# A graph attention kernel on one core: lookups of 128 edges with edges on partitions in place of edges on columns

## What is computed

```python
def _tconv(x, src, dst, ea, Wq, bq, Wk, bk, Wv, bv, We, Ws, bs):
    q = (x @ Wq + bq).reshape(n, H, C)
    k = (x @ Wk + bk).reshape(n, H, C)
    v = (x @ Wv + bv).reshape(n, H, C)
    e = (ea @ We).reshape(-1, H, C)
    kj = k[src] + e
    alpha = jnp.einsum('ehc,ehc->eh', q[dst], kj) / jnp.sqrt(jnp.float32(C))
    amax = jax.ops.segment_max(alpha, dst, num_segments=n)
    ex = jnp.exp(alpha - amax[dst])
    denom = jax.ops.segment_sum(ex, dst, num_segments=n)
    w = ex / (denom[dst] + 1e-16)
    msg = (v[src] + e) * w[:, :, None]
    out = jax.ops.segment_sum(msg, dst, num_segments=n).reshape(n, D)
    return out + x @ Ws + bs

x = _layernorm(x + _L0_gnn_ref(x, edge_attr_128, ...), axis=-1)
x = _layernorm(x + _L1_gnn_ref(x, edge_index, edge_weight, ...), axis=-1)
```

## Time and profile before

| | |
|---|---|
| median of 3 runs | 3948.93 us (3940.69 to 3951.46) |
| span of the profiled execution | 3951.6 us, beside 3951.46 us as its run's time |
| busy: PE, DVE, ACT, POOL | 2901.8, 1768.9, 1423.2, 2014.0 us |
| DMA packets | 407.14 MB, mean 103 GB/s |
| gathers of the attention stages | 1792, 943 ns each |

### The profile page before, as it was taken

How to read it: one execution, slowest core, us unless ns; L and a number is a source line. 1 busy time by engine, 2 the same in 40 slices (tenths; PEclk the granted TensorE clock), 3 DMA queues, 4 the chain that set the end, 5 groups by cost and what they waited for, 6 DMA issues and landing times. The chain is left out here.

```text
span 3951.6 us, 85365 instructions
## 1 busy us (share of the span) xinstructions
PE 2901.8 (73%) x20525; PEld 2444.9 (62%) x20525; DVE 1768.9 (45%) x5708; ACT 1423.2 (36%) x4457; POOL 2014.0 (51%) x2395
## 2 busy tenths in 40 slices
PE   4666999577777777777777875776777776777777
PEld 3445999466666666666666654665666665666655
DVE  5453445243444444344344872443444343434456
ACT  1001444233333333333333652333333333333357
POOL 5200111355665665566564665655666555665533
PEclk6557999677777877777888996778777777787889
DMA  7895322333333333333333662333333333333320
GB/s 206 269 266 177 85 83 82 85 88 91 90 91 89 90 92 89 90 91 90 89 90 73 155 151 79 90 90 90 91 91 90 90 89 88 92 90 92 87 45 25
DMA packets 527894, 407.14 MB, mean 103 GB/s; under 512 B 195972, under 2 KB 495412, under 8 KB 527464
## 3 DMA queue, kind: packets, MB, share of 16 engines
q1 hardware_dynamic: 413544, 282.02, 24.5%
q0 software_dynamic: 64768, 124.04, 12.9%
q10 hardware_dynamic: 49536, 0.55, 0.7%
HBM read 333.73 MB, written 72.56 MB: 103 GB/s over the span
## 5 line engine op out<-in xcount | busy, mean ns | idle before, releaser
L1359 POOL DMA_INDIRECT a_ring<-xg,edge x1792 | 1690.5, 943 | 1147.1 <-issue 524.3
L1410 PE MATMUL bank<-a_ring,a_weight_t 128*128 128x130 f32 x3584 | 707.2, 351 | 208.4 <-DVE acc_all L1515 178.3
L1497 DVE TENSOR_REDUCE a_bound<-bank 128x4 f32<-128x512 f32 x448 | 308.3, 688 | 1198.1 <-remote 1089.2
L1410 PEld LDWEIGHTS bank<-a_ring,a_weight_t 128*128 128x128 f32 x3584 | 608.5, 246 | 281.0 <-DVE acc_all L1515 230.3
L1515 DVE SCALAR_TENSOR_TENSOR acc_all<-acc_all,a_decay,bank 128x130 f32 x1792 | 627.6, 350 | 323.1 <-issue 46.3
L1373 PE MATMUL bank<-ident,a_ring 128*128 128x128 f32 x1792 | 350.9, 318 | 146.9 <-issue 120.9
L1383 PE MATMUL bank<-a_shared 17*128 17x128 bf16 x1792 | 234.4, 238 | 253.3 <-issue 252.6
L1391 PE MATMUL bank<-a_x_t,a_query 128*128 128x128 f32 x1792 | 336.7, 335 | 92.6 <-issue 74.7
L1464 ACT ACTIVATE a_weight_t<-bank 128x512 f32<-128x512 f32 x448 | 271.6, 606 | 352.2 <-remote 187.0
L1453 ACT ACTIVATE a_x_t<-bank,a_run 128x128 f32<-128x128 f32 x896 | 255.4, 368 | 392.5 <-DVE a_run L1500 276.5
L1391 PEld LDWEIGHTS bank<-a_x_t,a_query 128*128 128x128 f32 x1792 | 279.7, 233 | 151.2 <-issue 108.9
(11 more groups left out here) (276 smaller groups left out, 4063.4 us busy)
## 6 DMA issues: line engine op xcount, KB each, us to landing
a_query<-rec SPq DMA_DIRECT2D x896, 128.0 KB
c_ring<-in_edge_attr SPq DMA_DIRECT2D x344, 192.0 KB
a_ring<-xg,edge POOLq DMA_INDIRECT x1792
rec<-u_q_scores SPq DMA_DIRECT2D x98, 256.0 KB
rec<-p_q_scores SPq DMA_DIRECT2D x98, 256.0 KB
a_shared<-nrows SPq DMA_DIRECT2D x896, 8.5 KB
a_shared<-crows SPq DMA_DIRECT2D x224, 28.0 KB
c_node<-drec ACTq DMA_DIRECT2D x344, 1.5 KB
```

What stands on the lines that cost most here:

```text
L1359: pool.indirect_dma_start(out=ring[:, k, t, 0:FEAT], out_offset=None, in_=rows_of[:, :], in_offset=bass.IndirectOffsetOnAxis(ap=tiles_of(k ...
L1410: last = pe.matmul(sum_bank(t), weight_t[k % 2][:, t * P:(t + 1) * P], ring[:, k, t, :], start=True, stop=True)
L1497: dve.tensor_reduce(bound[:, k, :, STEPS - 1:STEPS].rearrange("q t s -> q (t s)"), score_bank(k), AX.X, ALU.max, negate=True).then_inc(max ...
```

## The change

The change replaces `attend_stage` and what feeds it. The edges of a tile now stay on partitions throughout.

- **Tiles.** A window is 128 nodes. 32 tiles are a group (`G`) of 8 slots of four tiles (`QUADS`), a layer has 26 groups (`NG`), so 208 slots and 832 tiles.
- **Gathers.** POOL gathers rows of 1 KB, key and value of a source node side by side (L1329), into a buffer of two groups. A slot's gathers wait for the sums of the same slot two groups earlier.
- **Queries.** SP spreads the places of a group's edges over 128 partitions (twice 512 KB per group). DVE makes from them a matrix of zeros and ones (L1471, 128 by 2048, bf16, two per group). PE multiplies it with the window's queries, which are kept in SBUF in three bf16 parts: 12 products of 132 columns per slot, each with a register instruction for its window (L1352).
- **Scores.** DVE multiplies the queries in PSUM with the gathered keys (L1479, 128 by 512) and sums 32 channels (L1482).
- **Maximum.** It is no longer carried tile by tile. Once per group a chain of 16 DVE instructions (`add_edges`, `scan_lanes`, `scan_tiles`, `sink`, `share`, `sink_sums`) finds the running maxima along lanes and tiles, with transposes and small products of PE and exponentials of ACT between them. It runs one group behind.
- **Sums.** DVE multiplies the gathered values by the exponentials (L1539, 128 by 4 by 128, both operands in SBUF). PE transposes the zeros and ones (L1359 of the changed file), ACT copies them, and PE makes the sums of 136 columns (L1371). DVE adds them to the window's without a factor (L1564).
- **Elsewhere.** The update and project stages write 388 key, value and query columns and 128 narrow ones in place of the folded queries and their terms. The project and output stages take means without `mix_heads`, and the 196 stores of L996 are gone. `count_stage` writes other tables.

The core of the diff:

```diff
-WN = HC
-NWIN = NW * GW
+G = 32
+QUADS = G // QUAD
+NG = -(-(NT + NW) // G)
+QW = FEAT + HEADS
+KV = 2 * FEAT
+SW = 2 * HEADS + FEAT
...
         @block.gpsimd
         def _(pool):
-                pool.wait_ge(summed, halves(at, k + 1))
-                for t in range(QUAD):
-                    pool.indirect_dma_start(
-                        out=ring[:, k, t, 0:FEAT], out_offset=None, in_=rows_of[:, :],
+                for q in range(QUADS):
+                    at.wait(summed, 2 * QUADS, 2 * (q + 1) - 4 * QUADS)
+                    for n in range(q * QUAD, (q + 1) * QUAD):
+                        pool.indirect_dma_start(
+                            out=ring[:, at.b, n, :], out_offset=None, in_=kv[:, :],
...
-                    last = pe.matmul(score_bank(k)[:, t, :], query[:, k % QS, t, :], x_t[k % XS][:, t * P:(t + 1) * P],
+                for t in range(QUAD):
+                    for s in range(SPLIT):
+                        rows = q3[:, bass.ds(held[q % 2 * QUAD + t], 1), s, :].rearrange("p a c -> p (a c)")
+                        last = pe.matmul(query_out(q)[:, t, :], hot_t[:, b, q * QUAD + t, :], rows, start=(s == 0),
...
-                dve.tensor_reduce(bound[:, k, :, STEPS - 1:STEPS].rearrange("q t s -> q (t s)"), score_bank(k), AX.X, ALU.max,
-                    dve.scalar_tensor_tensor(here, here, decay[:, k, t:t + 1], sum_bank(t), ALU.mult, ALU.add
+                dve.tensor_tensor(product[:, :, :], query_out(q)[:, :, 0:FEAT], ring[:, at.b, here, 0:FEAT], ALU.mult
+                                  ).then_inc(multiplied, 1)
...
+                dve.tensor_tensor(values, values, repeat(here[:, :, LEAD:LEAD + HEADS].unsqueeze(3), 3, HC), ALU.mult
+                                  ).then_inc(weighted, 1)
...
+                    dve.tensor_tensor(here, here, sum_out(t), ALU.add).then_inc(added, 1)
+            def step(at):
+                for s in range(QUADS):
+                    if s == 0 and linking:
+                        add_edges(at, b)
+                    if at.has():
+                        scores(at, s)
+                    if s == 1 and linking:
+                        scan_tiles(at, b)
+                    if s == 2 and linking:
+                        share(at, b)
...
+                        add(at, back, q)
...
+                        weigh(at, back, q)
+                    if s == 0 and linking:
+                        scan_lanes(at, b)
+                    if s == 1 and linking:
+                        sink(at, b)
```

More of the change, by code:

```diff
@@ L1245, in _, with __init__, has, count @@
             emit(NW - 1, (NW - 1) % 2)
[L1246 to L1254 removed]
+class Turn:
+    def __init__(self, eng, d, r=None):
+        self.eng, self.d, self.r, self.known = eng, d, r, {}
+        self.b = d % 2
+        self.now = d if r is None else r * 2 + d
+    def has(self, back=0):
+        return self.r is not None or 0 <= self.d - back < NG
+    def count(self, per, c):
+        if self.r is None:
+            return per * self.d + c
+        if (per, c) not in self.known:
+            self.known[per, c] = self.eng.snap(self.r * (2 * per) + (per * self.d + c))
+        return self.known[per, c]
+    def wait(self, sem, per, c):
+        if self.r is not None or per * self.d + c > 0:
+            self.eng.wait_ge(sem, self.count(per, c))
+    def wait_pair(self, sem, per, back=0):
+        half = per // 2
+        self.wait(sem, half, per - half * back - half * ((self.d - back) % 2))
+def turns_of(eng, step):
+    for g in (0, 1):
+        step(Turn(eng, g))
+    with eng.Fori(1, (NG - 2) // 2) as r:
+        for d in (0, 1):
+            step(Turn(eng, d, r))
+    for g in range(NG - 2, NG + 2):
+        step(Turn(eng, g))
+def windows_at(nc, m, eng, first, count=2 * QUAD):
+    here = m["wins"][0:1, bass.ds(first, count)]
+    _, values = nc.values_load_multi_w_load_instructions(
+        here, engines=[eng.engine], min_val=0, max_val=NW - 1,
+        skip_runtime_bounds_check_because="the count stage lists windows that there are")
+    return values
+def attend_stage(nc, m, layer):
+    bank, psum, ident, ident_bf, ones, low, lane, q3, ring, acc = (m[k] for k in (
+        "bank", "psum", "ident", "ident_bf", "ones", "low", "lane", "q3", "ring", "acc"))
+    kv, trec, places, breaks, links = m["kv"][layer], m["trec"], m["places"], m["breaks"], m["chain"]
+    LAG, WIDTH = 3, G + 1
+    SUMMED, ENDED, ENTERED, SUNK, SHARED, LINKS = 2, 4, 10, 13, 14, 16
     with ExitStack() as c, ExitStack() as inner:
@@ L1366, in _ @@
+            turns_of(pool, step)
         @block.tensor
         def _(pe):
[L1368 to L1384 removed]
@@ new lines, in grow, with step @@
+            def grow(at, b):
+                at.wait(below_ps, 1, 0)
+                act.activation(ring[:, b, :, LEAD:LEAD + HEADS], grown_out.rearrange("p (h t) -> p t h", h=HEADS), ACT.Exp
+                               ).then_inc(grown, 1)
+            def step(at):
+                linking = at.has(1)
+                for s in range(QUADS):
+                    if at.has():
+                        edge_parts(at, s)
+                    if s == 1 and linking:
+                        enter_columns(at, 1 - at.b)
+                    back, q = after(s)
+                    if at.has(back):
+                        copy_hot(at, back, q)
+                    if s == 1 and linking:
+                        grow(at, 1 - at.b)
```

1710 lines of the change are left out of this document (790 added, 920 removed).

## The result

The changed kernel takes 4049.74 us (median of 4 runs, 4035.34 to 4051.8), beside 3950.19 us for the one before in the same comparison. The ratio is 1.025, with a 95% interval of 1.0227 to 1.0273: slower, where the forecast said 3706 us and faster. The profiled execution of the changed kernel took 4035.34 us, its span is 4033.5 us.

The account below looks back on a forecast made before the run. POOL's gathers, stopping as before, with DVE close behind, were taken to bound attention: 26 x 49.6 + 54 = 1344 us per layer, 2687 for two, plus 1021 for other stages, gave 3708 us (3706 beside the median); range 3240 to 4330.

Parts of the forecast that it names:

- PE bounds it: Update stage: PE, busy 373 of 397 us, sets the time; fewer projection columns bring 397 to 387 us.
- Pace of the steady part: Attention: POOL's gathers, with stops as now, take 1.55 us each, 49.6 us per group of 32; chance 0.40.
- rival 1: Attention: gathers run without stops, 40.0 to 40.8 us per group, kernel 3251 us; chance 0.18.
- the chain's latency: Attention: waits between the linking chain's steps, covered by other DVE work, cost nothing; without cover 3 us per group.
- the sign that the forecast named for it: Attention: DVE waiting for PE or ACT at L1515 to L1533 would show the linking chain's cover was wrong.
- DVE's sum: Attention: DVE's work added up to 38.7 us per group, 4.84 per slot, close behind the gathers.
- Head and tail: Each attention layer: 6 us until first rows arrive and 48 us at the end, 54 us together.
- The direction's own test: Attention above 1463 us per layer would make the forecast direction, faster, wrong.
- No stops: Attention: slowness comes from SP's many transfers and PE's long program, so gathers run unbroken; kernel 3251 us; chance 0.18.
- Port lock: Attention: DVE's two-SBUF-operand and fast bf16 steps hold up POOL's gathers, 7.2 us per group; kernel 3583 us; chance 0.12.
- DVE behind the slow stretch: Attention: DVE can't work in the late 5.7 us of each gather burst; group 61.6 us, kernel 4332; chance 0.27.
- rival 3: Attention: DVE's doubled work is added to each burst's slow 5.7 us; kernel slower, 3960 up to 4330 us; chance 0.27.

Follow-up runs that it names:

- Experiment 1: Changed kernel with ACT taking the second part of the query split before its square root in the update stage: 3962.32 us, ratio 0.9884 to the kernel before.
- experiment 2: Changed kernel with DVE weighing the gathered values before it adds the last slot's sums in attention: 3932.81 us, ratio 0.9802 to the kernel before.
- experiment 5: Changed kernel with two of the four DVE additions of each slot left out (half of the sums missing): 4012.7 us.
- experiment 6: Changed kernel with the edits of Experiment 1 and experiment 2: 3808.13 us; adding a POOL lead of two slots in a layer's first two groups: 3730.33 us.
- experiment 4: Lookups replaced by plain transfers of the same bytes from fixed rows: changed kernel 3320.4 us (SP starts them) or 3308.65 (POOL); kernel before 2707.88 us.
- experiment 7: Experiment 6's two-edit kernel with a small POOL instruction behind each gather: 3940.93 us; with every second lookup a plain transfer: 3040.36; with 512-byte rows: 3785.13.
- the best version: Changed kernel with both order edits and POOL held to two slots ahead in a layer's first two groups: 3730.33 us, ratio 0.9443 to the kernel before.

## Why the prediction was wrong, point by point

The kernel took some 325 us more than the sum of 3708 (by the span of 4033.5). Of these, 206 are attention's (2893.2 beside 2687), 116 the update stage's, 24 the project stage's, and output, count and collect gave 21 back. Two steps failed, and the sign needed both: with either one as forecast the kernel would have come out below 3951.

**Update: "PE bounds it", 387 us.** The forecast said that PE bounds this stage and that 397 falls to 387 us. It measured 502.6. The step looked at how much work PE loses and not at what the change adds to the other queues: two splits on ACT and two subtractions on POOL, put ahead of a copy that PE waits for. In attention the forecast asked who waits for whom, and here it did not. Experiment 1 shows the price, 125 us of 502.6; what is left, 377.1, is near the forecast. Without it the change takes 1.2% less than the kernel before (0.9864 to 0.9903).

**Pace of the steady part.** The forecast's 49.6 us per group measured 52.76, so 82 us too little per layer. Its reading was right in kind: stops as before and not rival 1, at about the old rate per lookup, for a reason that is in the gathers. The step that failed is the cost of order: the chain's latency and the position of the additions were costed at nothing. Moving the weighing ahead of the additions gave back some 3 us (experiment 2), about the whole of the miss. The chain's share was not tested; the sign that the forecast named for it is there but small, DVE waiting for PE at L1515 (25.7 us) and for ACT at L1526 (18.9), 1.7 us per group. DVE's sum was on the high side, 38.7 forecast beside 30.9 busy, in part because busy time leaves out the gaps between additions (four take 1.61 us in the timeline and 1.18 busy), and this did little harm, as DVE's amount of work sets little (experiment 5).

**Head and tail.** These were put at 54 us with 6 until work begins. The first linking came 111.5 us into the stage, because POOL's buffer of 16 slots lets it make 61 gathers in one go, and rows 5 had shown what an unbroken row of gathers does to DVE. The forecast used that row against rival 1 and did not follow it into its own head. Together with the tail the error is 21 us per layer (1447 beside 1344, less 82). The lead of two at the head alone gave back 27 us of the time to the first linking (experiment 6).

**Project and output.** 165 forecast and 189.3 measured, inside its bounds; 130 and 121.8. **Count and collect** came out 12.4 us below the 339.

**The direction's own test.** "Attention above 1463 us per layer" was to make the direction wrong. Attention stayed at 1447, and the direction was wrong all the same, since the test took the other stages as settled at 1021 us; they took 1140.3.

**The rivals.** *No stops* fell: the lookups slow the others in the new stage as in the old. Its condition, that SP's transfers and PE's program are the reason, is answered by experiment 4, where the old kernel kept both and ran 1248 us faster. *Port lock* fell as the setter of pace: it asked for 7.2 us per group, while the gathers' mean grew by 46 ns, 1.5 us for 32 of them, and DVE's step of two SBUF operands was no longer than the one with an operand in PSUM (686 ns both). The Trainium skill (SBUF — State Buffer, "SBUF: two separate sides") has descriptor writing starve during VectorE's fast modes. The trace does show a small price where the forecast looked for it: 191 of the 1664 gathers took over 1.05 us, and 186 of them ran beside DVE's product of two SBUF operands (L1539, 154) or its bf16 comparison (L1471, 32); of the gathers beside neither, 1109, only 5 were so long. Most are stretched by 0.1 to 0.5 us, the longest, 3.3 us, stands in the head, and no run isolates it. *DVE behind the slow stretch* had the right sign for another reason: in the new stage DVE does work beside the gathers (30.9 us of a group), and halving its additions gave at most 1.8 of 4.7 us per group. Its 4332 us was not reached because the slow stretch is no fixed time to be added to DVE's work.

**What stays open.** Where the time goes is seen, in late hand-overs from one engine to the next while lookups follow one another 1.25 us apart. Which part of a lookup makes them late was not settled, nor whether scattered rows have a part in it. The measured 4050 us lies inside the forecast's range by luck: the range reached that far for rival 3, and what brought the kernel there was the update stage and the order in attention.

## What to carry to other kernels

When a change adds steps to an engine that is not the bottleneck, walk down that engine's queue and name each instruction that now stands behind them, and who waits for it; a stage that "PE bounds" can lose a quarter to one in-order wait (125 of 502.6 us here). When engines with time to spare all wait for one another, replace the suspected operation by one of the same size without its special part (here a plain transfer for a lookup): it shows within one run what all the waits come from. When a run meant to help comes out slow, ask again what sets its pace: the pauses of experiment 7 freed the other engines and made POOL the slowest. A redesign that leaves the number of lookups nearly as it is, 832 for 896, and their spacing too, could save little here, whatever it took off the engines.

## What the runs showed of the hardware that was not expected

- A gather of 128 rows by index keeps POOL busy for 0.95 us and the next can start after 1.25, and yet no kernel whose every transfer is a lookup got below 1.60 us for each: 1.60 before, 1.74 after, 1.63 in the best version.
- The same transfer without indices is 0.55 us of POOL and leaves no late hand-over: 3308.65 us for the whole kernel in place of some 4105 at the same level (1.025 times 4005.21), and 2707.88 in place of 3955.88 for the one before.
- Beside an unbroken row of lookups PE, DVE and ACT did no instruction in 28.2 us. PE's last product ended at 863.66, and its increment of the semaphore for ACT came at 891.98. With a small POOL instruction between lookups, so that they start 1.46 us apart and not 1.25, the late starts of ACT's copy fall from 869 to 15 us, and at one lookup in 2.35 us there is none. POOL then sets the pace in the first case, 54.6 us per group against 51.6.
- Row length did not matter: 512 and 1024 bytes gave the same group time within the level of the runs.
- Gathers over 1.05 us (191 of 1664) stood beside DVE's product of two SBUF operands or its bf16 comparison in 186 cases; at a mean of 989 ns in place of 943 the price is 1.5 us per group.
- PE standing still for 2 us in every 10 cost more than the 2 us: the granted clock fell from 0.98 to 0.87 and the mean of a 128 by 128 product (L965) rose from 276 to 322 ns.
